# One exp call for each pair of score banks in the attention loop

## The reference

```python
q = apply_axial_rope((x @ Wq).reshape(b, n, 32, 16), pos_map)
k = apply_axial_rope(k.reshape(b, ctx_n, 32, 16), ctx_pos_map)
logits = jnp.einsum('bqhd,bkhd->bhqk', q, k) * scale
w = jax.nn.softmax(logits, axis=-1)
attn = jnp.einsum('bhqk,bkhd->bqhd', w, v).reshape(b, n, 512)
return attn @ Wout + bout
```

## Time and profile before

| | |
|---|---|
| median of the runs | 1331.42 us |
| the profiled execution | 1335.91 us |
| its span, first to last instruction | 1334.1 us |
| mean granted clock of TensorE | 0.955 |
| TensorE matmul busy | 1174.2 us (88%) |
| VectorE busy | 830.4 us (62%) |
| ScalarE busy | 666.2 us (50%) |
| GpSimd busy | 397.7 us (30%) |
| score matmuls of the attention, first to last | 676.9 to 1195.2 us |

### The profile page before, as it was taken

The page is one execution under the profiler, slowest core; times in us unless marked ns, Lnnn a source line. Parts: engine busy times, 40 slices in busy tenths (PEclk is TensorE's granted clock), DMA queues, the critical chain, the costliest instruction groups (busy, mean ns, idle before and its releaser), DMA issues.

```text
span 1334.1 us, 16599 instructions
## 1 busy us (share of the span) xinstructions
PE 1174.2 (88%) x5308; PEld 511.9 (38%) x5309; DVE 830.4 (62%) x1283; ACT 666.2 (50%) x1175; POOL 397.7 (30%) x469
## 2 busy tenths in 40 slices
PE   5776876897999999958799989999999999889998
PEld 3454443564444444423232223222322222234543
DVE  6787865244455554135988888778777777624543
ACT  2575564564222222235456666566656556662453
POOL 4455631001222222033234432222223233101332
PEclk8988997999899999977999999999999999998999
DMA  7324125654444444194324342222222225300011
GB/s 247 129 91 134 56 95 195 223 192 159 150 147 154 147 147 135 56 277 112 113 85 132 116 124 72 85 81 81 68 85 80 81 81 66 46 0 9 33 40 48
DMA packets 111029, 145.79 MB, mean 109 GB/s; under 512 B 24952, under 2 KB 79736, under 8 KB 110440
## 3 DMA queue, kind: packets, MB, share of 16 engines
q1 hardware_dynamic: 91816, 113.47, 26.6%
q0 software_dynamic: 18368, 28.85, 8.4%
q10 hardware_dynamic: 768, 2.49, 0.5%
HBM read 99.54 MB, written 48.37 MB: 111 GB/s over the span
## 4 chain that ended last, share of the span: by engine, by line
PE 33%; DVE 8%; issue 8%; ACT 7%; POOL 1%; DMA 0%; ACTq 0%; POOLq 0%; DVEq 0%
PE PS L2864 8%; PE PS L2830 6%; PE PS L2765 5%; PE PS L2849 4%; PE PS L2789 3%; DVE a_top L3191 3%; ACT shared_w L2986 3%; PE PS L2368 2%; ACT a_E L2986 2%; PE PS L2391 1%; PE PS L1961 1%; POOL a_K L2128 1%; DVE a_early L3071 1%; PE PS L2759 1%; DVE X L3139 0%
## 5 line engine op out<-in xcount | busy, mean ns | idle before, releaser
L3191 DVE TENSOR_REDUCE a_top<-PS 128x2 f32<-128x1024 f32 x256 | 308.8, 1223 | 89.5 <-PE PS L2849 83.2
L2830 PE MATMUL PS<-a_Q,a_K 99*128 99x512 bf16 (+1 forms) x512 | 167.5, 387 | 18.7 <-ACT a_E L2986 4.2
L2986 ACT ACTIVATE shared_w<-PS 128x512 f32<-128x512 f32 x256 | 138.8, 596 | 80.1 <-PE PS L2830 77.2
L2986 ACT ACTIVATE a_E<-PS 128x512 f32<-128x512 f32 x256 | 138.9, 596 | 63.0 <-PE PS L2830 59.7
L1481 PE MATMUL PS<-f_W,f_GT 128*128 x312 | 141.8, 598 | 0.0
L2849 PE MATMUL PS<-a_K,a_Q 64*128 64x512 bf16 x512 | 100.4, 389 | 7.8 <-DVE a_top L3191 7.2
L2830 PEld LDWEIGHTS PS<-a_Q,a_K 99*128 99x128 bf16 (+1 forms) x512 | 44.5, 98 | 155.2 <-issue 50.8
L1908 POOL TENSOR_TENSOR a_qf<-a_qf,a_tab 128x512 f32<-128x512 f32 x15 | 19.1, 1272 | 282.3 <-DVE a_swapped L3093 282.3
L1537 DVE TENSOR_TENSOR f_H<-f_SG,PS 128x256 f32<-128x256 f32 x39 | 16.4, 421 | 125.5 <-ACT f_SG L1521 125.5
L1481 PEld LDWEIGHTS PS<-f_W,f_GT 128*128 128x128 f32 x312 | 57.0, 193 | 57.3 <-issue 57.3
L2765 PE MATMUL PS<-a_xT,a_early 128*128 128x512 f32 x128 | 72.3, 661 | 2.1 <-ACT a_xT L2952 0.7
(11 more groups left out here) (379 smaller groups left out, 2058.1 us busy)
## 6 DMA issues: line engine op xcount, KB each, us to landing
f0r_raw<-in_L_ffn_W_dram SPq DMA_DIRECT2D x24, 512.0 KB, 4.5
a_K<-k_parts SPq DMA_DIRECT2D x192, 64.0 KB, 2.3
a_Q<-a_q_parts SPq DMA_DIRECT2D x186, 64.0 KB
f_y<-f_Y SPq DMA_DIRECT2D x39, 256.0 KB
v_units<-V SPq DMA_DIRECT2D x16, 512.0 KB, 2.9
a_V<-v_units SPq DMA_DIRECT2D x16, 512.0 KB, 3.6
k_parts<-f_k_parts SPq DMA_DIRECT2D x16, 384.0 KB, 3.4
a_q_parts<-a_parts SPq DMA_DIRECT2D x16, 384.0 KB, 2.8
```

Source lines behind the costliest of these rows:

```text
L2830: nc.tensor.matmul(PS[:, 4 + h % 2, :], K6[k][0:rows_, o, head // 2, kt * P:(kt + 1) * P], Q6[k][0:rows_, o, head // 2, :], start=True, st ...
L2986: nc.scalar.activation(E[step % 2][:, h, :], PS[:, 4 + h % 2, :], ACT.Exp).then_inc(exp_done, 1)
L3191: nc.vector.tensor_reduce(top[:, h - h % 2:h - h % 2 + 2, t], PS[:, 2 * pair:2 * pair + 2, :], AX.X, ALU.max).then_inc(maxed, 1)
```

## The change

`exps` loops no more over its two heads. It waits for the score of the second head of the pair, then for the E buffer as before, and issues one call that reads banks 4 and 5 (1024 columns) and writes both tiles of E. `exp_done` rises by two at the end of that call. All waits of other engines are as they were. The change is in the one function alone:

```diff
-                    for h in hs:
-                        act.wait_ge(st_done, n_st(unit, step, h))
-                        if h == 0 and not (is_first(unit) and step < 2):
-
-                            act.wait_ge(pv_done, n_unit(unit, 8) - 8 + step - 1)
-                        if h == 0 and is_first(unit) and step == 1:
-                            act.wait_ge(late.gated, late.N)
-                        nc.scalar.activation(E[step % 2][:, h, :], PS[:, 4 + h % 2, :], ACT.Exp).then_inc(exp_done, 1)
+                    act.wait_ge(st_done, n_st(unit, step, hs[1]))
+                    if hs[0] == 0 and not (is_first(unit) and step < 2):
+
+                        act.wait_ge(pv_done, n_unit(unit, 8) - 8 + step - 1)
+                    if hs[0] == 0 and is_first(unit) and step == 1:
+                        act.wait_ge(late.gated, late.N)
+                    nc.scalar.activation(E[step % 2][:, hs[0]:hs[0] + 2, :], PS[:, 4:6, :], ACT.Exp).then_inc(exp_done, 2)
```

## The result

The changed kernel takes 1357.94 us, the median of four runs (1356.43 to 1359.13), beside 1330.57 for the kernel before (four runs, 1329.64 to 1335.47). The ratio is 1.0194, 95% interval 1.0176 to 1.0212: slower, by 27 us where 20 were forecast. The profiled execution took 1358.77, its span is 1357.0.

The account below looks back on a forecast made before the run. The prediction took a loop of latencies between TensorE and ScalarE as the bound, with TensorE's queue setting the length. Gross loss 17.6 + 6.0 = 23.6 us, less 3.9 hidden, gives 1331.4 + 19.7 = 1351 us, range 1343 to 1362.

Parts of the forecast that it names:

- The sign and the mechanism: In attention, a slowdown: merged exp waits for both scores and releases both banks together; net 19.7 us.
- What bounds the stretch: Attention, 521 of 1334.1 us: TensorE and ScalarE wait for each other in turn; ScalarE is idle 36%.
- pairs without cover: Score pairs where TensorE lacks enough other work during the exp: 82 pairs, gross loss 23.6 us.
- The call's length: Merged exp of 1024 columns on ScalarE: 1.024 us taken, between 1.012 and 1.09.
- When the call starts: Merged exp on ScalarE starts 0.42 us after the pair's second score matmul starts.
- part (c): Slots where another ScalarE copy already delays the exps: 35 pairs at 0.17 us, 6.0 us.
- (a): Slots with no or nearly no other TensorE job: 33 pairs losing 0.375 us each.
- (b): Slots holding four transposes on TensorE: 14 pairs losing 0.37 us each.
- the cover: Slots with projection or query jobs, and each step's second pair: 1.82 and 1.86 us of work hide 1.72; no loss.
- VectorE's cover: TensorE's existing waits for VectorE's row maxima absorb some delay: 3.9 us back, between 0 and twice that.
- The clock: Rival: idle moments give each attention unit a half-clock TensorE stretch, 17 us more, 1368 us; chance 0.08.
- From profile to median: Whole-kernel time: the median lies 4.5 us below the profiled execution, so 19.7 is added to 1331.4.

Follow-up runs that it names:

- kernel that counts pairs: The changed kernel with the merged exp call raising its semaphore by one instead of two and TensorE's waits adjusted: 1352.74 us, ratio 1.014.

## Why the prediction was right, and by how much it was off

The sign and the mechanism held, the size was low by 7 us. That the range covers this is in part luck: its upper end rested in part on a longer call, which did not come, and on stretches at half clock in the last units, while two of the three that doubled lie in units 3 and 7.

- **What bounds the stretch.** Right for the pairs without cover. There TensorE and ScalarE wait in turn, and 14 us less work on ScalarE took nothing off; merged where there is cover, it changed nothing either (ratio 0.999). But the 101.1 us of waits that the prediction read for this are those of weight loads; the score matmuls themselves waited only 7.6 us for exps before the change. The Trainium skill (Perfetto Trace Analysis, Optimizing Scalar/DVE Operations) has it that an engine which is not saturated but makes others wait may be better off with smaller instructions. The trace agrees: the score matmuls' waits for exps went from 7.6 to 47.9 us with the larger ones.
- **The call's length.** Right. 1.024 was taken from a call of another line (L420), and 1.023 to 1.024 came out.
- **When the call starts.** Mis-sized: "It starts 0.42 after S1". It starts 0.46 after, since the wait left the call. In the typical unit that is 0.05 in slot 6 and 0.05 in slot 8, and nothing where a copy runs in front (the two places of part (c)): 1.17 for the 1.085 forecast. The kernel that counts pairs takes it away and has 1.09.
- **Parts (a), (b), (c) and the cover.** Followed step by step through unit 9 of the kernel that counts pairs, S3 falls behind by 0.16 over slots 4 and 5, 0.375 over 6 and 7, and 0.54 over 8 to 11: the prediction's 0.16, 0.37, and 0.375 + 0.17. Over all 16 units of that kernel S3 comes later behind its S0 by 0.36 to 0.39 in 41 steps and by 0.14 to 0.19 in 30, where the sums had 47 and 35 pairs, and by nothing in 42. Full slots and second pairs lost nothing, in the experiment that merged only these as well.
- **VectorE's cover.** Mis-sized: "I put back 0.8 for units 1 and 2 each and 1.3 for unit 3". The 13.0 us in 16 waits that it was taken from the earlier trace rows add the waits of matmuls and of weight loads: 4.5 us in 6 are the matmuls', the rest the weight loads'. Units 1 and 2 lost 1.65 and 1.28, not 1.03 each; unit 3 0.60 in the changed kernel but 1.18 where pairs are counted, for 0.53. Over these three that is 1.5 us in the kernel that counts pairs, of the 2.75 by which its attention (542.02, 22.45 over before) is above the 19.7 forecast. In unit 3 the cover can't be told from the clock, whose stretch moved there. Of the matmuls' waits for maxima (7.2 us in all 16 units) only 2.3 went in the changed kernel.
- **The clock.** As a rival it was wrong for the typical unit, which keeps a clock of 1.00 though TensorE stands idle there for up to 0.84 us at a time. The Trainium skill (TensorE: Matmul & The Clock Gate, A second HAM failure mode) tells of a clock that swings with brief idle moments between groups of matmuls; no such swing shows in this unit. But in the three units with a table change the stretches doubled, which the forecast had only in its range. Units 7 and 14 are 1.16 and 1.80 longer than where pairs are counted. Units 3 and 4 are 0.58 and 0.43 shorter than there, where the stretch from 807.01 reaches from the one into the other and makes unit 4's first step 0.96 longer. All units together make the 3.58 between 22.45 and 26.03.
- **From profile to median.** The prediction added 19.7 to a median of 1331.4, taking the 4.5 us between it and the profiled execution as the same for both kernels. The profile after is 0.8 above its median, the one before 5.3: the spans differ by 22.9 and the medians by 27.4.

Of the 7 us, then, 6.3 are in the attention (26.0 for 19.7), and the rest comes of this last step: 27.4 less 26.0 is 1.4, less the 0.8 by which the median of before fell with its fourth run.

## What to carry to other kernels

Before merging two calls on an engine that others wait for, find who waits for the first of them: the merged call starts with the later input and gives everything back at its end, and an engine that is idle for a third of the time saves nothing by one call in place of two. Where TensorE had other work up to 1.81 us after S0 the merge was free here; in an empty slot it cost what S3 shows, 0.375 us a pair. Let the merged call raise its semaphore by one and count calls. When a gap is found in such a loop, look for work queued behind the waiting instruction that could stand in front of it, and watch who must keep up with that work: in the typical unit it was VectorE.

## What the runs showed of the hardware that was not expected

A call on ScalarE that raises its semaphore by two started 0.096 us after the score's end (median), with its wait as a separate instruction in the trace; with a raise by one it started 0.037 after, with the wait in the call. A table load of 1.28 us in front of the call began only after the separate wait, and during the wait when this was in the call: the first exp came 1.97 us after its first score for 1.17. The stretches at half clock were 3.4 or 6.8 us long and repeated to 0.01 us when the same kernel ran again; behind waits of 2.36, 2.29 and 2.14 in the same place of three kernels they were 6.8, 3.4 and none, and one followed a wait of only 0.94.
